# Layer norm of a graph network fed from a transposed copy of its input, in place of transposes on TensorE

## What is computed

```python
def _layernorm(x, axis=-1, eps=1e-5):
    m = jnp.mean(x, axis=axis, keepdims=True)
    v = jnp.var(x, axis=axis, keepdims=True)
    return (x - m) / jnp.sqrt(v + eps)
...
# layer 0: graph attention, 8 heads of 64 units
h = jnp.maximum(_layernorm(x, axis=-1), 0.0)
feats = jnp.einsum('bnf,hfu->bhnu', X, W)            # X is h
e_self = jnp.einsum('bhnu,hu->bhn', feats, a_self)
e_neigh = jnp.einsum('bhnu,hu->bhn', feats, a_neigh)
dense = leaky_relu(e_self[..., :, None] + e_neigh[..., None, :]) + NEG_BIG * (1.0 - A)
out = relu(softmax(dense) @ feats + b)               # x = x + out
# layer 1: layer norm, relu, two hypergraph convolutions (512 -> 1024 -> 512), x = x + y
```

## Time and profile before

| | us |
|---|---|
| median of 3 runs | 2612.44 (2610.91 to 2613.1) |
| the profiled execution, its own time | 2612.08 |
| its span, first to last instruction | 2610.3 |
| PE busy | 2559.5 (98%) |
| DVE busy | 1880.3 (72%) |
| ACT busy | 1518.2 (58%) |
| POOL busy | 1458.9 (56%) |
| granted TensorE clock, mean | 0.995 of full speed |
| DMA queue, share of 16 engines | 18.0% |

### The profile page before, as it was taken

The page is one execution under the profiler, slowest core; times in us unless marked ns, Lnnn a source line. Parts: engine busy times, 40 slices in busy tenths (PEclk is TensorE's granted clock), DMA queues, the critical chain, the costliest instruction groups (busy, mean ns, idle before and its releaser), DMA issues.

```text
span 2610.3 us, 51365 instructions
## 1 busy us (share of the span) xinstructions
PE 2559.5 (98%) x15508; PEld 2245.7 (86%) x15508; DVE 1880.3 (72%) x4638; ACT 1518.2 (58%) x3593; POOL 1458.9 (56%) x2196
## 2 busy tenths in 40 slices
PE   4999999999999999999999999999999999999998
PEld 3888888888888888888888888888888888888886
DVE  6777777777777777777777777777777777777774
ACT  3565556556555555656655565565565555556553
POOL 5555555555555555555555555555555555555553
PEclk8999999999999999999999999999999999999999
DMA  4111111111111111111111111111111111111110
GB/s 151 52 55 62 58 60 63 58 60 55 66 60 55 63 58 60 62 59 60 55 62 59 60 63 58 60 57 64 60 54 62 58 60 63 58 60 55 65 51 25
DMA packets 85593, 158.70 MB, mean 61 GB/s; under 512 B 16832, under 2 KB 33216, under 8 KB 85568
## 3 DMA queue, kind: packets, MB, share of 16 engines
q1 hardware_dynamic: 85568, 158.39, 18.0%
HBM read 124.26 MB, written 34.08 MB: 61 GB/s over the span
## 4 chain that ended last, share of the span: by engine, by line
PE 96%; DVE 1%; issue 0%; ACT 0%; POOL 0%; POOLq 0%; DVEq 0%
PE p_w1a L793 14%; PE p_w1a L795 14%; PE p_w1a L794 14%; PE p_att L864 8%; PE p_w1b L793 5%; PE p_w1b L794 5%; PE p_w1b L795 5%; PE p_w1b L898 4%; PE p_att L844 4%; PE p_ta L811 4%; PE p_fa L794 2%; PE p_fa L795 2%; PE p_fa L793 2%; PE p_fb L794 2%; PE p_fb L793 2%; PE p_fb L795 2%
## 5 line engine op out<-in xcount | busy, mean ns | idle before, releaser
L359 POOL TENSOR_TENSOR rs<-ve,halfpow 128x1 f32<-128x1 f32 x128 | 115.0, 898 | 550.6 <-DVE ve L745 550.6
L793 PE MATMUL p_w1a<-W_hi,rT_hi 128*128 128x512 f32 x1024 | 414.8, 405 | 0.0
L794 PE MATMUL p_w1a<-W_lo,rT_hi 128*128 128x512 f32 x1024 | 403.7, 394 | 0.0
L795 PE MATMUL p_w1a<-W_hi,rT_lo 128*128 128x512 f32 x1024 | 403.5, 394 | 0.0
L424 ACT ACTIVATE att<-u,shifts 128x128 f32<-128x128 f32 x1024 | 400.3, 391 | 4.7 <-DVE shifts L705 4.7
L425 ACT ACTIVATE att_low<-u,shifts 128x128 f32<-128x128 f32 x1024 | 400.2, 391 | 0.0
L349 POOL TENSOR_TENSOR u<-u,mask 128x1024 f32<-128x1024 f32 x128 | 307.2, 2400 | 29.2 <-POOL mask L346 17.4
L319 POOL TENSOR_TENSOR ve<-mv,eps 128x1 f32<-128x1 f32 x256 | 93.0, 363 | 411.3 <-DVE mv L630 326.1
L477 ACT ACTIVATE rT_hi<-p_tb 128x512 fp32r<-128x512 f32 x128 | 76.7, 599 | 330.0 <-PE p_tb L811 330.0
L760 DVE SCALAR_TENSOR_TENSOR z<-p_w1a,rs,t_bc 128x512 f32<-128x512 f32 x128 | 96.1, 750 | 218.3 <-PE p_w1a L795 218.3
L864 PE MATMUL p_att<-feats,attT 128*128 128x65 f32 x2048 | 242.5, 271 | 2.2 <-ACT attT L467 2.2
(11 more groups left out here) (127 smaller groups left out, 7128.5 us busy)
## 6 DMA issues: line engine op xcount, KB each, us to landing
u<-en_rows SPq DMA_DIRECT2D x128, 512.0 KB, 3.6
x_in<-in_x SPq DMA_DIRECT2D x128, 256.0 KB, 2.6
out<-raw SPq DMA_DIRECT2D x128, 256.0 KB, 2.1
adj_in<-in_adj SPq DMA_DIRECT2D x128, 128.0 KB, 2.4
en_rows<-eT SPq DMA_DIRECT2D x512, 1.0 KB
raw<-in_W1T SPq DMA_DIRECT2D x2, 1024.0 KB, 11.0
raw<-in_W2T SPq DMA_DIRECT2D x2, 1024.0 KB, 9.8
raw<-in_W0T SPq DMA_DIRECT2D x1, 1024.0 KB, 6.5
```

Of the source, the lines that this page charges most:

```text
L359: nc.gpsimd.tensor_tensor(rs1[:, :], ve1[:, :], halfpow[:, :], ALU.pow).then_inc(s_rs1, 1)
L793: mm(dst, hi, w_hi, start=first, stop=False)
L794: mm(dst, hi, w_lo, start=False, stop=False)
L795: return mm(dst, lo, w_hi, start=False, stop=final)
```

## The change

A copy of x with features on partitions (`xT`) is made as a further input. SP loads 256 KB of it for each graph into `xT_in` (`load_xT`, two buffers). DVE's statistics are as before. The mean, one number per partition, is written to a row in DRAM (`mu_row`) and read back to all partitions (`mu_bc`), two DMAs on SP's queue with a wait between them. POOL subtracts it (`xc`, 128x512). ACT's relu and DVE's rest now read `xc` in SBUF and not PSUM, and stand elsewhere in their turns, one turn earlier; `h0` gets two buffers. POOL's product for the shift, ACT's `xn` and PE's four transposes go. The scale `rs0` is kept per graph (four columns) and multiplied in by DVE as a per-partition operand where it moves features and scores out of PSUM. `r`, `rest` and `z` move into `raw`, and the last piece of W2 is loaded later.

```diff
+            def load_xT(g):
+                if g.has(2):
+                    sp.wait_ge(s_xc, g.count(2))
+                n = g.base if g.loop is None else g.loop * UNROLL + g.base
+                sp.dma_start(xT_in[:, g.slot(2), :, :],
+                             xT[bass.ds(n, 1), :, :, :].rearrange("a p c n -> p (a c) n")).then_inc(s_xT[g.slot(2)], 16)
...
 SP, turn:
                     load(g)
+                if g.within(NG) and (g.loop is not None or g.base >= 2):
+                    load_xT(g)
...
+                g = t.plus(4)
+                if g.within(NG):
+                    sp.wait_ge(s_mv0, g.count())
+                    sp.dma_start(mu_row.rearrange("a n -> n a"), mv0[:, 0:1]).then_inc(s_mu_out, 16)
+                    sp.wait_ge(s_mu_out, g.count(per=16))
+                    sp.dma_start(mu_bc[:, :], mu_row.broadcast_to([P, N])).then_inc(s_mu_bc, 16)
                 g = t.plus(-1)
...
 POOL, turn:
-                    rstd(g, mv0, ve0, rs0, s_mv0, s_ve0, s_rs0, s_xn, nm0, s_nm0)
-                    shift(g, nm0, rs0, nb0, s_nm0, s_rs0, s_nb0)
+                    rstd(g, mv0, ve0, rs0[:, g.slot(4):g.slot(4) + 1], s_mv0, s_ve0, s_rs0)
...
+                g = t.plus(4)
+                if g.within(NG):
+                    pool.wait_ge(s_xT[g.slot(2)], g.uses(2, 16))
+                    pool.wait_ge(s_mu_bc, g.count(per=16))
+                    if g.has(1):
+                        pool.wait_ge(s_h0_lo, g.count(1))
+                    nc.gpsimd.tensor_tensor(xc[:, :, :], xT_in[:, g.slot(2), :, :],
+                                            mu_bc[:, :].unsqueeze(1).broadcast_to([P, DC, N]), ALU.subtract).then_inc(s_xc, 1)
...
 ACT, turn, behind attT:
+                    act.wait_ge(s_xc, g.count())
+                    nc.scalar.activation(h0[:, g.slot(2), :, 0, :], xc[:, :, :], ACT.Relu).then_inc(s_h0_hi, 1)
...
 DVE, turn:
-                    nc.vector.tensor_copy(e_blk[:, 0:EW], p_fa[:, D2:D2 + EW]).then_inc(s_e_blk, 1)
+                    nc.vector.tensor_scalar(e_blk[:, 0:EW], p_fa[:, D2:D2 + EW], scale, None, ALU.mult).then_inc(s_e_blk, 1)
...
-                        nc.vector.tensor_tensor(feats[:, g.slot(2), b * HH:(b + 1) * HH, 0:UN],
+                        nc.vector.scalar_tensor_tensor(feats[:, g.slot(2), b * HH:(b + 1) * HH, 0:UN],
...
 DVE, turn, behind ve1 and nm1:
+                    dve.wait_ge(s_h0_hi, g.count())
+                    nc.vector.scalar_tensor_tensor(h0[:, g.slot(2), :, 1, :], xc[:, :, :], 0.0, h0[:, g.slot(2), :, 0, :],
+                                                   ALU.max, ALU.subtract).then_inc(s_h0_lo, 1)
...
 PE, turn, at its end:
-                    pe.wait_ge(s_xn, g.count())
...
-                    transposes(p_ta, xn, s_xnT)
```

More of the change, by code:

```diff
@@ L62, in turns, with gnn_two_layers @@
         turn(Graph(t))
-def gnn_two_layers(nc, x, adj2, W0T, b0, a_self, a_neigh, W1T, b1, gammaT, betaT, W2T, b2, out):
+def gnn_two_layers(nc, x, xT, adj2, W0T, b0, a_self, a_neigh, W1T, b1, gammaT, betaT, W2T, b2, out):
     NG, N, D = x.shape
@@ L162, in gnn_two_layers @@
         s_in = [sem(f"s_in{i}") for i in range(4)]
+        s_xT = [sem(f"s_xT{i}") for i in range(2)]
         s_out = [sem(f"s_out{i}") for i in range(2)]
@@ L243, in _ @@
             load(Graph(0))
+            load_xT(Graph(0))
             load_piece(0)
@@ L256, in _ @@
             load(Graph(2))
-            load_piece(4)
             load(Graph(3))
@@ L278, in turn, with setup_last @@
                     sp.dma_start(out[bass.ds(n, 1), :, :].rearrange("a p d -> p (a d)"), y[:, g.slot(2), :]).then_inc(s_out[g.slot(2)], 16)
-            turns(sp, turn, NG)
+            def setup_last():
+                load_piece(4)
+            turns(sp, turn, NG, {-2: setup_last})
             for i in range(2):
@@ L429, in turn @@
             def turn(t):
[L430 to L436, removed]
                 if t.plus(1).within(NG):
@@ L444, in turn @@
                     nc.scalar.activation(r[:, 0:HALF], r[:, 0:HALF], ACT.Relu).then_inc(s_r, 1)
-                g = t.plus(4)
-                if g.within(NG):
-                    act.wait_ge(s_nb0, g.count())
-                    if g.has(1):
-                        act.wait_ge(s_xnT, g.count(1))
-                    nc.scalar.activation(xn[:, :], x_in[:, g.slot(4), :], ACT.Identity, bias=nb0[:, :],
-                                         scale=rs0[:, :]).then_inc(s_xn, 1)
                 g = t
@@ L468, in turn @@
                                          ACT.Copy).then_inc(s_attT_sb, 1)
+                g = t.plus(4)
+                if g.within(NG):
+                    act.wait_ge(s_xc, g.count())
+                    if g.has(2):
+                        act.wait_ge(s_feats, g.count(2))
+                    nc.scalar.activation(h0[:, g.slot(2), :, 0, :], xc[:, :, :], ACT.Relu).then_inc(s_h0_hi, 1)
                 if t.base == -1:
@@ L628, in turn @@
                     dve.wait_ge(s_stats0, t.plus(4).count())
+                    if t.plus(4).has(1):
+                        dve.wait_ge(s_ve0, t.plus(4).count(1))
                 if t.plus(4).within(NG):
@@ L824, in turn @@
                     pe.wait_ge(s_r, g.count(per=2) - 1)
-                    if g.plus(3).within(NG):
-                        pe.wait_ge(s_h0_lo, g.plus(3).count())
+                    if g.has(1):
+                        pe.wait_ge(s_rT_lo, g.count(1, per=2))
                     transposes(p_ta, r[:, 0:HALF], s_rT)
@@ L855, in turn @@
                     for c in range(2):
-                        features(c, 0)
-                        features(c, 1)
+                        features(g, c, 0)
+                        features(g, c, 1)
                 g = t.plus(1)
@@ L888, in turn @@
                 if g.within(NG):
-                    features(2, 0)
+                    features(g, 2, 0)
                 g = t.plus(1)
@@ L902, in turn @@
                 if g.within(NG):
-                    features(2, 1)
-                    features(3, 0)
-                    features(3, 1).then_inc(s_feats, 1)
+                    features(g, 2, 1)
+                    features(g, 3, 0)
+                    features(g, 3, 1).then_inc(s_feats, 1)
                 g = t.plus(2)
```

73 lines of the change are left out of this document (36 added, 37 removed).

## The result

The changed kernel takes 3597.78 us (median of 4 runs, 3590.47 to 3605.78) against 2611.68 us before (4 runs): 1.378 times as long, 95% interval 1.3752 to 1.3804. The forecast was 2690.

A forecast was written before the change was run, and what follows sets the result against it. PE was taken as the bound, with 96% of the chain that ended last. 2612.1 + 20.0 (start) - 7.4 (transposes) + 65.5 (POOL's meeting with L684) = 2690 us; the 8-in-10 range was 2613 to 2740.

The forecast's parts named there:

- the mean by DMA: Mean's write and read back in the loop: lands about 1310.6, ahead of `u`'s end, so `xc` waits for `u`.
- Rival B: No port meeting in the loop: mean lands after 1311.15, or L684 gets in before `xc`; 2625 us, chance 0.28.
- the covers: ACT's relu and DVE's `h0_lo` go ahead of waits for PE of 2.6 and 1.7 us a turn, costing nothing.
- the highest: Rival C's upper form: more meetings, and POOL's third 1/sqrt also waits, some 0.5 us a turn; 2752 us, chance 0.11.
- the prediction's own signs: In the changed kernel's profile, L684 staying at 0.15 us or `xc` waiting for DMA in the loop would mean rival B.
- POOL's meeting with L684: `xc` right behind `u` holds DVE's small L684 on the shared port: 0.88 us in 60% of 124 turns, 65.5 lost.
- PE's 7.4 us: Turn's end, transposes gone: PE's weight load moves up 0.06 us behind `hg_lo` in 124 turns, 7.4 us gained.
- The start: Before the loop: POOL's products for W0 wait behind graph 0's mean and `xc`, starting 20 us later.
- The scale in the features: DVE, three per-partition operations ahead of `eT`: 0.18 us that costs PE nothing, with `eT` 0.24 us later.
- the loads of x^T: SP's queue at 18%: 256 KB more a turn costs nothing within the loop.
- DVE's rest: `h0_lo`, 0.69 us, goes ahead of DVE's 1.7 us wait for PE at `z`: costs nothing.

The follow-up runs named there:

- with late readers: Changed kernel with slow mean transfers kept, but `xc`, ACT's relu and DVE's rest moved back to the next turn's start: 2680.85 us.
- with rows: Changed kernel, whole computation, with the mean put through DVE's 32x32 transpose and written as four rows of 128 bytes: 2644.76 us.
- Without the transfers and the meeting: Changed kernel with zeros for the mean, no mean transfers, and DVE's 128x2 limit of the counts split into two 128x1 instructions: 2618.64 us.
- the split wait: PE waits for `hg_lo` only ahead of the third matmul: 2641.79 us on top of late readers, 2609.24 alone on the kernel before.

## Why the prediction was wrong, point by point

**The step that failed is the mean by DMA.** The prediction took the write as landed behind `u`'s data and the read as 1.5 us, bounded by 0.9 and 3.3, and concluded that "`xc` waits for `u` and not for the mean. That is a matter of half a microsecond." The two legs measured 7.4 and 4.7 us, and `xc` waited 6.3 for the mean behind `u`. The bounds came from transfers that were larger or of fewer pieces; none of the rows had many pieces in one 512-byte stretch, so the write had no upper bound at all, and its landing behind `u`'s data was taken without a row. Rival B tried 1 us more for the write's small pieces, where 5 were due. The prediction cites beside it the Trainium skill, "DMA: Bandwidth & Descriptors", section "Specifications": transfers under 512 bytes are done as read, modify, write. The runs show that size alone does not decide: 128 pieces of 4 bytes land in 2.7 us when apart, and four of 128 bytes into the same 512 in 1.9.

**With it the covers went.** That ACT's relu costs nothing ahead of a wait of 2.6 us held only while `xc` is on time; with `xc` 6.3 us late the cover of 2.6 was used up and ACT waited 7.93. The prediction said what the cover was worth but never asked what else could make the relu late; rival B priced a late mean as a gain (no meeting), up to any lateness. Priced by the chain of the earlier trace rows, a mean 6 us late is 6 - 2.6 = 3.4 us and more a turn, over 400 us, and that case was in no rival, of which the highest gave 2752. The clock's fall in the wait (2.05 us a turn) was not in it either. By the prediction's own signs (`xc` waits for DMA, L684 stays at 0.15) the run is rival B, with 2625.

**POOL's meeting with L684: right without the transfers, with its size off.** In the changed kernel it does not occur, since `xc` comes too late for it. Without the transfers it occurs as told, with `xc` starting where `u` ends. The term was 0.88 us in 60% of 124 turns, 65.5 us; measured are 111 of 129 instances (86%) and 78 us (2696.63 less 2618.64), 0.70 for each. That 2696.63 lies near the forecast of 2690 is luck: the meeting took more than its term, and the start, 3.9 us late without a mean to wait for, less.

**PE's 7.4 us: the load moved up as told, the time did not come.** The load starts 0.053 us behind `hg_lo` where it was 0.112, and waits the 0.30 that were forecast; with late readers the turn is still 19.81 against 19.79 before, for the rest of the turn is some 0.1 longer.

**The start: right in kind, too small.** 20 us were forecast, 57 measured. For graph 0 the working came near: its write was sent at 18.18 for a forecast 17.0, its read back at 30.59 for 27.9, and the products for W0 began at 35.95 for 31.0. But it looked at graph 0 alone. Each of the first four graphs waits for its own two legs, SP waits in between, and the last piece of W2 stands behind two of them. Without the transfers the start is 3.9 us late, with the write spread out (and no read) 20.9, with rows 26.7.

**The scale in the features, the loads of x^T, DVE's rest.** Nothing in these runs speaks against the "nothing" that was put on them: without the transfers and the meeting the kernel is at 2618.64, 7 above before, of which 3.9 are the start.

## What to carry to other kernels

A transfer whose row the trace does not have (many tiny pieces, one line of memory) has no upper bound from other transfers: put it where a long latency is covered, or price the case in which it is late by the first wait behind it. Where an engine works in order, a wait for a DMA round trip belongs behind the other work of its turn: the same transfers of some 12 us cost 7.4 us in the median turn with the readers early and 0.02 with them late. Work taken from the engine that bounds the kernel is worth its time only if the chain that ran beside it is shortened too: the 0.36 us of the transposes came only with the split wait.

## What the runs showed of the hardware that was not expected

A write of 128 pieces of 4 bytes into 512 contiguous bytes of DRAM is reported done 7.4 us after its issue, in the turn shown 5 us after its last packet; spread 512 bytes apart it takes 2.7, as four pieces of 128 bytes 1.9. A read of those bytes behind the slow write takes 4.6 us in place of 3.0, behind the write of four rows 2.9. A read of 512 KB beside the slow write is in single turns reported landed over 5 us after its issue, in the turn shown 9.5, which is 6 us after its last packet. A 128x2 limit on DVE that meets a POOL operation on 128x512 is held for that one's whole rest (1.10 us), a 128x1 is not (0.14). PE's granted clock falls to 0.50 inside a wait of 4.4 us, stands at 0.51 over the 5.2 us behind it and is back at 1.00 in the next stretch.
